# Two edits in a chain of eight layers: the quantised layer's fp32 matmuls as fp32r triples, and the totals of the output projections in parts of 2 and 6 batches

## The chip, the cores and the metric

The kernel runs on one core of one Trainium2 chip. The metric is the device time of one launch in microseconds (us). The core's engines are named as in the profile: PE is TensorE's matmul, PEld its weight load, DVE VectorE, ACT ScalarE, POOL GpSimd, and SP the engine that issues most DMAs. PSUM is the memory that TensorE writes its sums to, in banks of 512 fp32 columns.

## The reference, cut to what matters

The network is a stream x of 8 sequences of 512 tokens and 256 features, to which four attention layers and four feed-forward layers are added in turn. The first feed-forward layer is the quantised one. All its activations are rounded to a grid of 16 bits that is set by the largest absolute value of the whole tensor, and its weights to 4 bits in blocks of 32:

```
def act_qdq(x):
    scale = max(max(abs(x)) / 32767, 1e-12)
    return clip(round(x / scale)) * scale

h    = act_qdq(layernorm(x))                        # 4096 tokens x 256
gate = act_qdq(h @ lpbq_dequant(w_gate).T)          # 4096 x 768
up   = act_qdq(h @ lpbq_dequant(w_up).T)            # 4096 x 768
sig  = round(sigmoid(gate) * 65536), at most 65535, / 65536
act  = act_qdq(gate * sig)
y    = act_qdq(act * up) @ lpbq_dequant(w_down).T   # 4096 x 256
```

Each maximum is over the whole tensor, so a stage can't start before the one ahead of it has ended.

Each attention layer ends in an output projection: the unnormalised heads are multiplied by the reciprocals of the softmax totals (16 or 8 heads for each token), and then by a 256 x 256 matrix, and the result is added to x.

## The kernel before, in words

The program is a row of phases. Each ends in a barrier of all engines, so phases don't overlap and their times add up. Within a phase every engine has its own program, in an order written out by hand, and waits on semaphores. NB is 8 batches of S = 512 tokens, KT = 2 halves of the 256 features, FT = 6 tiles of 128 hidden features, P = 128 and W2 = 256.

**The quantised layer** is these phases. `f1w` (`dequantise`, line 1311) loads the three weights, rounds them on DVE, then transposes them in 36 blocks of 128 x 128 on PE, each copied out of PSUM by ACT (lines 1360 and 1366). `f1n` normalises, `f1g`, `f1h`, `f1i` and `f1j` turn maxima into scales, `f1t` rounds and transposes the activations into `gridT` (code name xT). `f1a` does the gate and up products, PE in tiles of 128 x 512 (lines 1404 and 1408), two fp32 matmuls for each tile; ACT copies each gate tile to the tensor `hidden` (code name act_, line 1417), DVE takes the maximum of each up tile (line 1425) and, for each batch, of the gate tiles (line 1429). The up product isn't kept. `f1b` rounds the gate, takes its sigmoid on ACT, rounds that on DVE and multiplies (lines 1449 to 1464). `f1c` does the up product again, in half batches of 256 tokens: PE (line 1515), ACT scales each tile out of PSUM and adds MAGIC (a float that makes the addition round to a whole number, line 1527), ACT the same for the gated hidden values (line 1528), DVE subtracts MAGIC and scales both (lines 1544 and 1546), multiplies them (line 1552) and takes the maximum (line 1539). `f1d` is the down product. In `f1a` and `f1c` the loops over batches are loops on the engines (`Fori`).

**The output projection** (`outproj`, line 958) runs four times, as `o0`, `o1`, `o3` and `o7`. SP loads the totals in two parts, batch 0 and batches 1 to 7. DVE takes the reciprocals of a part and splits them in an upper and a lower half in fp32r (`split`, lines 1106 to 1110; both parts stand ahead of all its other work), SP writes the halves to DRAM (`spread`, line 1017) and reads them back with heads on partitions (`collect`, line 1022). PE spreads each batch's rows over the features by matmuls with `sel` (`spread`, line 1046), DVE multiplies the heads by them (`scale`, line 1117), ACT rounds that to fp32r (line 1075), DVE subtracts to get the lower half (`lower`, line 1122), and PE multiplies (`project`, line 1056). PE's order is `spread(0)`, then for each b `spread(b + 1)` and `project(b)`. DVE's is `split(0)`, `split(1)`, `scale(0)`, `lower(0)`, and for each b `scale(b + 1)`, `add(b - 1)`, `lower(b + 1)`. The feature halves of a batch of heads are loaded to `xT`, which has three buffers (`load`, line 1007).

## Time and profile before

| | |
|---|---|
| time, median of 3 runs | 5969.54 us (5959.56 to 5976.63) |
| the profiled execution: its own time | 5963.57 us |
| its span | 5961.9 us |
| PE busy | 4522.7 us (76%) |
| DVE busy | 3866.3 us (65%) |
| ACT busy | 2895.7 us (49%) |
| POOL busy | 2017.2 us (34%) |
| moved by DMA | 648.19 MB, 109 GB/s on average |

The shares of busy time are averages over many phases with different limits, so what a change in one phase is worth is read in that phase. The profiled execution took 1.7 us more than its span. The granted clock of TensorE is given as a share of 2.4 GHz: 1.00 is 2.4 GHz, 0.50 is 1.2 GHz, and a figure between them is a stretch with both.

### The profile page before, as it was taken

The numbers are of one execution on the slowest core, as the hardware profiler recorded it, in microseconds if no ns is written. First come the engines' busy times: TensorE is split into PE (matmuls) and PEld (weight loads), VectorE is DVE, ScalarE is ACT, GpSimd is POOL, SyncE is SP. The second block draws the span as 40 slices with busy tenths as digits, with TensorE's granted clock in tenths as the row PEclk, the third lists the DMA queues.
The fourth block names the chain that finished last, engine by engine and source line by source line (L and its number), as shares of the span: only waits on it lengthen the run. The fifth ranks groups of instructions, "written<-read, shape, count | busy, mean of one in ns | idle before, by whom it ended". The sixth has DMA issues, their size and how long they took to land. (4 is left out here: it accounts for less than half of the span.)

```text
span 5961.9 us, 94850 instructions
## 1 busy us (share of the span) xinstructions
PE 4522.7 (76%) x24898; PEld 2823.5 (47%) x24898; DVE 3866.3 (65%) x8219; ACT 2895.7 (49%) x6148; POOL 2017.2 (34%) x3169
## 2 busy tenths in 40 slices
PE   7677764837789739986768676988676987995897
PEld 3333442336433318872236455876455853334434
DVE  6566665395478754443779776569665556885565
ACT  2566642251277533234546566346565324772363
POOL 0344420000366312223435542235541216532342
PEclk9899987969899869997779899999899998997897
DMA  6889950000633202105522321013321044323533
GB/s 224 302 308 309 315 202 16 0 0 5 203 93 93 77 20 65 43 28 135 149 73 110 133 72 42 15 44 124 117 68 32 8 139 130 89 67 113 169 118 102
DMA packets 327033, 648.19 MB, mean 109 GB/s; under 512 B 73202, under 2 KB 140435, under 8 KB 326632
## 3 DMA queue, kind: packets, MB, share of 16 engines
q1 hardware_dynamic: 259544, 463.30, 23.5%
q0 software_dynamic: 67104, 180.70, 10.4%
q8 instruction: 126, 2.06, 0.1%
q14 instruction: 259, 2.12, 0.1%
HBM read 361.41 MB, written 251.28 MB: 103 GB/s over the span
## 5 line engine op out<-in xcount | busy, mean ns | idle before, releaser
L828 DVE TENSOR_REDUCE t_nmax<-t_aps 128x2 f32<-128x1024 f32 x700 | 837.8, 1221 | 278.0 <-PE t_aps L750 272.5
L935 ACT ACTIVATE t_expT<-t_bps 128x512 f32<-128x512 f32 x1290 | 701.3, 599 | 284.9 <-PE t_bps L769 235.1
L769 PE MATMUL t_bps<-t_Q,t_K 51*128 51x512 f32 (+2 forms) x1290 | 526.0, 470 | 60.1 <-ACT t_expT L935 43.9
L750 PE MATMUL t_aps<-t_K,t_Q 49*128 49x512 f32 (+2 forms) x1400 | 465.3, 460 | 63.5 <-DMA t_K<-k_halves 27.9
L769 PEld LDWEIGHTS t_bps<-t_Q,t_K 51*128 51x128 f32 (+2 forms) x1290 | 229.2, 190 | 526.8 <-ACT t_expT L935 373.9
L2112 DVE TENSOR_TENSOR f_hl<-f_h,f_hh 128x512 fp32r<-128x512 f32 x192 | 203.3, 1059 | 409.7 <-ACT f_hh L2037 409.7
L796 PE MATMUL t_ops<-t_expT,t_V 128*17 128x512 f32 (+1 forms) x2560 | 414.4, 615 | 0.4 <-ACT t_expT L935 0.4
L3549 ACT ACTIVATE t_relsb<-t_relsb,t_nmax 128x128 f32<-128x128 f32 (+3 forms) x512 | 288.8, 564 | 221.8 <-DVE t_nmax L3521 221.0
L3427 POOL TENSOR_TENSOR t_relsb<-t_relsb,t_M 128x128 f32<-128x128 f32 x512 | 216.6, 454 | 388.8 <-DMA t_relsb<-rel 388.7
L2404 POOL TENSOR_TENSOR a_crossed<-a_qsb,a_tab 128x256 f32<-128x256 f32 x272 | 262.2, 985 | 251.6 <-ACT a_qsb L2351 218.8
L3180 ACT ACTIVATE t_prob<-t_summed,t_nmax,norms 128x256 f32<-128x256 f32 (+1 forms) x560 | 317.4, 571 | 39.1 <-DVE t_nmax L3239 29.1
L869 POOL DMA_DIRECT2D t_Q<-q_halves x525 | 270.9, 518 | 144.2 <-POOLq L78 74.2
L3456 PE MATMUL t_tps<-ident,t_relsb 128*128 128x128 f32 x1280 | 249.1, 296 | 59.9 <-ACT t_expT L3348 59.8
L3120 PE MATMUL t_tps<-ident,t_prob 128*128 128x128 f32 x964 | 147.6, 298 | 179.3 <-DVE t_prob L3253 179.3
L3521 DVE CUSTOM_DVE_ANT_0 t_relsb<-t_sps,t_relsb 128x128 f32<-128x128 f32 (+3 forms) x512 | 245.9, 482 | 49.3 <-POOL t_relsb L3427 48.9
L869 POOL DMA_DIRECT2D t_K<-k_halves x525 | 267.5, 511 | 17.2 <-issue 8.9
L3468 PE MATMUL t_rps<-t_erk,t_Q 96*128 96x512 bf16 (+3 forms) x512 | 168.4, 332 | 129.9 <-ACT t_rows L3355 69.5
L750 PEld LDWEIGHTS t_aps<-t_K,t_Q 49*128 49x128 f32 (+2 forms) x1400 | 215.0, 199 | 103.0 <-issue 51.7
L3191 ACT COPY t_expT<-t_tps 128x512 f32<-128x512 f32 (+1 forms) x276 | 144.3, 523 | 205.0 <-PE t_tps L3120 205.0
L3456 PEld LDWEIGHTS t_tps<-ident,t_relsb 128*128 128x128 f32 x1280 | 174.7, 153 | 131.8 <-ACT t_relsb L3549 100.1
L1977 PE MATMUL f_yps<-f_wdh,f_hh 128*128 128x256 f32 x768 | 217.7, 283 | 13.8 <-DVE f_hl L2112 13.8
L3348 DVE COPY t_expT<-t_tps 128x128 f32<-128x128 f32 (+1 forms) x256 | 107.9, 422 | 176.1 <-PE t_tps L3456 176.0
(445 smaller groups left out, 12410.3 us busy)
## 6 DMA issues: line engine op xcount, KB each, us to landing
rel<-t_rows SPq DMA_DIRECT2D x128, 640.0 KB, 4.6
t_relsb<-rel SPq DMA_DIRECT2D x128, 640.0 KB, 6.3
t_Q<-q_halves POOLq DMA_DIRECT2D x420, 64.0 KB, 2.5
t_K<-k_halves POOLq DMA_DIRECT2D x420, 64.0 KB, 2.5
k_halves<-a_parts SPq DMA_DIRECT2D x48, 512.0 KB, 4.8
q_halves<-a_parts SPq DMA_DIRECT2D x48, 512.0 KB, 5.6
o_xT<-attended SPq DMA_DIRECT2D x32, 512.0 KB, 4.1
f_R<-combine SPq DMA_DIRECT2D x128, 128.0 KB, 2.9
```

The lines of the kernel that those rows point to most:

```text
L750: last = nc.tensor.matmul(aps[:, (t * PPG + i) % 2, x, :], operand(Qr, KA, p, h, slice(t * P, (t + 1) * P)), operand(Kr, KA, p, h, slice(0 ...
L769: nc.tensor.matmul(bps[:, slot_of(kb, j), :], operand(Kr, KB, p, h, slice(kb * P, (kb + 1) * P)), operand(Qr, KB, p, h, slice(0, S)), star ...
L796: last = nc.tensor.matmul(ops[j * COL:j * COL + VW, :], V[:, p, kb, g * HG + j, :], expT[:, kb % RING, j, :], start=kb == 0, stop=kb == NT ...
L828: nc.vector.tensor_reduce(nmax[:, g, t, i * HPT:(i + 1) * HPT], aps[:, (t * PPG + i) % 2], AX.X, ALU.max, negate=True).then_inc(s["maxed"], 1)
L869: pool.dma_start(dst[o + i * DH:o + (i + 1) * DH, p, cols], rows(src, part, r, g, b)).then_inc(sem, 16)
L935: nc.scalar.activation(expT[:, kb % RING, j, :], bps[:, slot_of(kb, j), :], ACT.Exp).then_inc(s["expo"], 1 + (PAD if end else 0))
L1977: last = nc.tensor.matmul(o, fast(x), fast(w), start=m == 0 and i == 0 and t % 2 == 0, stop=m == NF - 1 and i == 2, skip_group_check=True)
L2404: last = nc.gpsimd.tensor_tensor(y[:, :, k, :], x[:, :, 1 - k, :], tab[:, 2 * i + 1, t, k * HW:(k + 1) * HW].unsqueeze(1).broadcast_to([P, ...
L3180: nc.scalar.activation(prob[:, u.slot, i, x, 0:w], summed[:, u.slot, i, x, 0:w], ACT.Exp, scale=rn[:, ds(u.b * NT + t, 1), h:h + 1].rearra ...
L3456: last = nc.tensor.transpose(tps[:, t % 2, kb * P:(kb + 1) * P], tile(n, t)[:, kb * P:(kb + 1) * P], G.ident[:, :])
L3521: nc.vector.tensor_tensor_reduce(out=tile(n, t), in0=sps[:, u % SB, 0:WIDTH[t]], in1=tile(n, t), scale=1.0, scalar=3.0e38, op0=ALU.add, op ...
L3549: nc.scalar.activation(tile(n, t), tile(n, t), ACT.Exp, scale=-1.0, bias=nmax[:, n % RING, t:t + 1]).then_inc(s["expo"], 1)
```

## The change

**Matmuls.** Where `f1a` and `f1c` multiplied in fp32, each operand now stands in two fp32r parts, the upper one rounded and the lower one the rest, and three fp32r matmuls take the place of one fp32 matmul (upper x upper, lower weight x upper, upper weight x lower; `triple`). The weight parts are made in `f1w`, the upper by ACT's copy and the lower by a subtraction on DVE; the transposes go by groups of three or four to a PSUM bank, with four banks in use instead of two. The activation parts are made batch by batch in `f1a`, and again in `f1c`: the upper by an ACT copy of 128 x 1024 (`upper`), the lower by DVE in chunks of 128 x 512 into a ring of three (`lower`).

**f1a** is unrolled and uses four banks each for gate and up where it used two. **f1b** rounds the sigmoid in one DVE instruction fewer for each half batch. **f1c** works on tiles of 512 tokens, its scales are folded so that the up values need no pass of their own on DVE, and ACT scales the hidden values two batches ahead. **outproj** has parts of 2 and 6 batches, `load(0)` is issued ahead of the weight, and PE waits for the second part at `spread(2)`.

```diff
@@ outproj
-        PARTS = ((0, 1), (1, NB))
+        PARTS = ((0, 2), (2, NB))
...
                 totals(0)
+                load(0)
                 sp.dma_start(W[:, :, :], w).then_inc(s["w"], 16)
                 totals(1)
-                spread(0)
-                load(0)
-                collect(0)
                 if bias is not None:
                     sp.dma_start(B[:, :], bias.broadcast_to([P, D])).then_inc(s["b"], 16)
+                spread(0)
+                load(1)
+                collect(0)
                 spread(1)
-                load(1)
+                load(2)
                 collect(1)
-                load(2)
...
-                    if b < 2:
-                        pe.wait_ge(s[f"rows{b}"], 16)
+                    for i, (first, _) in enumerate(PARTS):
+                        if b == first:
+                            pe.wait_ge(s[f"rows{i}"], 16)
@@ dequantise
-        wps = ps("wps", [P, 2, S])
+        wps = ps("wps", [P, 4, S])
...
+                for n, (srcs, hi, lo) in enumerate(turns()):
+                    if lo is not None:
+                        dve.wait_ge(s["copied"], n + 1)
+                        nc.vector.tensor_tensor(lo.bitcast(F32R), wps[:, n % 4, 0:len(srcs) * P], hi, ALU.subtract).then_inc(s["lower"], 1)
...
+                for n, (srcs, hi, lo) in enumerate(turns()):
+                    if n >= 4:
+                        pe.wait_ge(s["lower" if n - 4 < 8 else "copied"], n - 3)
+                    for m, src in enumerate(srcs):
+                        last = nc.tensor.transpose(wps[:, n % 4, m * P:(m + 1) * P], src, G.ident[:, :])
+                    last.then_inc(s["turned"], 1)
@@ quantised_ffn, helpers of f1a and f1c
+        def triple(pe, s, o, wh, wl, xh, xl, b, m):
+            cols = slice(m * P, (m + 1) * P)
+            for i, (w, k) in enumerate(((wh, 0), (wl, 0), (wh, 1), (wl, 1))):
+                nc.tensor.matmul(o, fast(w[:, k, cols]), fast(xh[:, b % 2, k]), start=i == 0, stop=False)
+            for k in range(KT):
+                if m == 0:
+                    pe.wait_ge(s["lo"], b * KT + k + 1)
+                last = nc.tensor.matmul(o, fast(wh[:, k, cols]), fast(xl[:, (b * KT + k) % 3]), start=False, stop=k == KT - 1)
+            return last
+        def lower(dve, s, xh, xl, c):
+            b, k = divmod(c, KT)
+            if b < NB:
+                dve.wait_ge(s["hi"], b + 1)
+                if c >= 3:
+                    dve.wait_ge(s["u"], ((c - 3) // KT + 1) * FT)
+                nc.vector.tensor_tensor(fast(xl[:, c % 3]), xT[:, k, b * S:(b + 1) * S], xh[:, b % 2, k], ALU.subtract).then_inc(s["lo"], 1)
@@ f1a, DVE
+                    for c in range(3):
+                        lower(dve, s, xh, xl, c)
+                    for b in range(NB):
                         for m in range(FT):
...
+                            nc.vector.tensor_reduce(mx[:, 1, n:n + 1], ups[:, n % 4, :], AX.X, ALU.max, apply_absolute_value=True).then_inc(s["u_mx"], 1)
+                        for c in (b * KT + 3, b * KT + 4):
+                            lower(dve, s, xh, xl, c)
...
@@ f1b, DVE
-                            nc.vector.tensor_scalar(sg[:, x], sg[:, x], 65536.0, MAGIC, ALU.mult, ALU.add).then_inc(s["weighed"], 1)
+                            nc.vector.tensor_scalar(sg[:, x], sg[:, x], 65535.0 / 65536.0, MAGIC / 65536.0, ALU.min, ALU.add).then_inc(s["weighed"], 1)
...
-                            nc.vector.tensor_scalar(sg[:, x], sg[:, x], MAGIC, 65535.0, ALU.subtract, ALU.min).then_inc(s["weighed"], 1)
+                            nc.vector.scalar_tensor_tensor(half(i, x), sg[:, x], MAGIC / 65536.0, half(i, x), ALU.subtract, ALU.mult).then_inc(s["weighed"], 1)
...
-                            nc.vector.scalar_tensor_tensor(half(i, x), sg[:, x], 1.0 / 65536.0, half(i, x), ALU.mult, ALU.mult).then_inc(s["weighed"], 1)
@@ f1c, ACT
+                    def upper(b):
+                        if b >= 2:
+                            act.wait_ge(s["u"], (b - 1) * FT)
+                        nc.scalar.copy(fast(xh[:, b % 2]), xT[:, :, b * S:(b + 1) * S]).then_inc(s["hi"], 1)
...
+                    upper(0)
+                    upper(1)
                     act.wait_ge(s["set"], 1)
+                    scaled(0)
+                    scaled(1)
+                    for b in range(NB):
+                        if b:
+                            act.wait_ge(s["product"], b * 2)
+                        for m in range(FT):
...
+                            nc.scalar.activation(up[:, m, :], ups[:, n % 4, :], ACT.Identity, scale=G.quant[:, 1, 1:2], bias=magic[:, 0:1]).then_inc(s["u_cp"], 1)
+                            if m == 1 and 1 <= b < NB - 1:
+                                upper(b + 1)
+                        if b + 2 < NB:
+                            scaled(b + 2)
@@ f1c, DVE
+                    for c in range(3):
+                        lower(dve, s, xh, xl, c)
+                    whole(0, 0)
+                    whole(0, 1)
+                    for b in range(NB):
+                        lower(dve, s, xh, xl, b * KT + 3)
+                        product(b, 0)
+                        product(b, 1)
                         for x in range(2):
+                            if b + 1 < NB:
+                                whole(b + 1, x)
+                            largest(b, x)
+                        lower(dve, s, xh, xl, b * KT + 4)
```

`whole` is one tensor_scalar of 128 x 1536, `product` one scalar_tensor_tensor of 128 x 1536 that also takes MAGIC off the up values, `largest` the maximum of 128 x 1536, each for a half batch.

## Rows read from the trace of the kernel before

**Rows 1.** Windows over f1a and f1c: busy us (count) by engine, PEclk, DMA share, GB/s.

```profile
1005.00:1173.00 168.00, 165.06 (x384) 72.90 (x384) 57.05 (x56) 28.08 (x48) 0.00 (x0) 1.00 0.00 0
...
1283.00:1376.00 93.00, 85.28 (x384) 74.28 (x383) 82.82 (x64) 73.64 (x112) 0.00 (x0) 0.96 0.00 0
```

The engines of a window's row are PE, PEld, DVE, ACT and POOL, in this order. A line of the timeline has the start (us), the duration (us), engine, line, operation, tiles, and in brackets the idle time before it with what ended it.

**Rows 2.** Timeline of f1a: PE's first matmul, its last weight load, the tail.

```profile
1005.41 1.98 PE L1404 MATMUL f1a_gps<-gridT,gateT 128*128 x4 [2.28 <-ACTq L1413]
...
1169.46 0.19 PEld L1408 LDWEIGHTS f1a_ups<-gridT,upT 128*128 128x128 f32 x1 [0.24 <-issue]
...
1170.62 0.69 DVE L1425 TENSOR_REDUCE mx<-f1a_ups 128x512 f32 x1 [2.74 <-PE f1a_ups L1408]
```

**Rows 3.** Timeline of a later layer: fp32r matmuls of 512 columns, weight loads 1 and 9.

```profile
4803.26 0.19 PEld L1963 LDWEIGHTS f_gps<-f_xh,f_wgh 128*128 128x128 f32 x1
...
4805.09 0.19 PEld L1963 LDWEIGHTS f_ups<-f_xh,f_wul 128*128 128x128 f32 x1
```

**Rows 4.** Tile f_hl (ns min/median/max), and groups of ACT lines (busy us, mean ns).

```profile
L2112 DVE TENSOR_TENSOR f_hl<-f_h,f_hh x192: 691/694/2554, 2253.7 to 4807.9; 128x512 fp32r<-128x512 f32 x192
...
L1527 ACT ACTIVATE f1c_up<-f1c_ups,f1c_magic,quant 128x256 f32<-128x256 f32 x96 | 50.1, 560 | 29.1 <-PE f1c_ups L1515 29.1
...
L1477 ACT ACTIVATE hidden<-hidden,f1b_magic,quant (+1 forms) x16 | 25.6, 1653 | 8.2 <-DVE f1b_magic L1466 8.2
...
L2021 ACT CAST f_xh<-f_x 128x1024 fp32r<-128x1024 f32 x16 | 16.8, 1047 | 1.2
```

**Rows 5.** Timeline of f1b, DVE: the pair that the change removes, and the next.

```profile
1213.09 1.82 DVE L1458 TENSOR_SCALAR f1b_sg<-f1b_sg 128x1536 f32<-128x1536 f32 x2
1214.83 3.42 DVE L1461 SCALAR_TENSOR_TENSOR hidden<-f1b_sg,hidden 128x1536 f32 x2
```

**Rows 6.** Timeline of f1c: PE's start, three operations of DVE, its last.

```profile
1282.63 17.65 PE L1515 MATMUL f1c_ups<-gridT,upT 128*128 x69 [112.16 <-PEq L1509]
...
1321.40 1.75 DVE L1552 TENSOR_TENSOR hidden<-hidden,f1c_up 128x1536 f32 x1
...
1323.07 1.01 DVE L1544 TENSOR_SCALAR f1c_up<-f1c_up,quant 128x1536 f32<-128x1536 f32 x1
...
1323.99 1.01 DVE L1546 TENSOR_SCALAR hidden<-hidden,quant  x1
...
1375.05 1.75 DVE L1539 TENSOR_REDUCE mx<-hidden 128x1 f32<-128x1536 f32 x1
```

**Rows 7.** Window of 1 us in f1c, PE alone: busy, then PEclk.

```profile
1287.00:1288.00 1.00, 1.00 (x4) 0.64 0.00 0
```

**Rows 8.** Timeline of transposes: f1w's, its last copies, and f1t's first.

```profile
936.33 14.80 PE L1360 MATMUL f1w_wps<-ident,f1w_raw 128*128 128x128 f32 x36 [32.28 <-DVEq L1340]
...
950.95 0.48 ACT L1366 COPY downT<-f1w_wps 128x128 f32<-128x128 f32 x2 [0.35 <-PE f1w_wps L1360]
...
990.97 3.51 PE L1272 MATMUL f1t_xps<-ident,f1t_rows 128*128 128x128 f32 x16 [39.84 <-DVE f1t_rows L1255]
```

**Rows 9.** Timeline of o0: second reciprocal, lower(0), rows of part 2, project(0).

```profile
859.04 2.95 DVE L1106 RECIPROCAL o_rs<-o_rs 128x448 f32<-128x448 f32 x1 [1.65 <-DMA o_rs<-sums]
...
865.18 1.23 DVE L1122 TENSOR_TENSOR o_xl<-o_xn,o_xh 128x1024 fp32r<-128x1024 f32 x1 [0.68 <-ACT o_xh L1075]
...
871.52 1.19 PE L1046 MATMUL o_rps<-o_rows,o_sel 32*128 32x512 f32 x2 [8.10 <-DMA o_rows<-o_inverse]
...
872.64 0.58 PE L1056 MATMUL o_yps<-o_Wh,o_xh 128*128 128x256 f32 x1
```

**Rows 10.** Timeline of o1: lower(0) and the start of project(0).

```profile
2056.12 2.34 DVE L1122 TENSOR_TENSOR o_xl<-o_xn,o_xh 128x1024 fp32r<-128x1024 f32 x1 [0.68 <-ACT o_xh L1075]
...
2063.38 0.58 PE L1056 MATMUL o_yps<-o_Wh,o_xh 128*128 128x256 f32 x1
```

**Rows 11.** Timeline of o7: the same two.

```profile
5903.90 1.23 DVE L1122 TENSOR_TENSOR o_xl<-o_xn,o_xh 128x1024 fp32r<-128x1024 f32 x1 [0.68 <-ACT o_xh L1075]
...
5908.41 0.58 PE L1056 MATMUL o_yps<-o_Wh,o_xh 128*128 128x256 f32 x1
```

More of the change, by code:

```diff
@@ L1496, in quantised_ffn, with piece @@
         grid(nc, G, "f1i", [mx[:, 3, 0:2 * NB]], [3])
-        with phase(nc, "f1c", "u u_cp pre set whole product") as (s, psb, ps):
-            up = psb("up", [P, 2, FT, W2])
+        with phase(nc, "f1c", "hi lo u u_cp pre set whole product peak") as (s, psb, ps):
+            up = psb("up", [P, FT, S])
+            xh = psb("xh", [P, 2, KT, S])
+            xl = psb("xl", [P, 3, S])
             magic = psb("magic", [P, 1])
+            both = psb("both", [P, 1])
             ups = ps("ups", [P, 4, S])
+            def piece(b, x):
+                return act_[:, :, b * S + x * W2:b * S + (x + 1) * W2]
@@ L1518, in _ @@
                 @block.scalar
                 def _(act):
-                    def batch(b, first=False):
-                        for x in range(2):
-                            if not first:
-                                act.wait_ge(s["product"], b * 2 + x - 1)
-                                alone(act)
-                            for m in range(FT):
-                                act.wait_ge(s["u"], b * (2 * FT) + x * FT + m + 1)
-                                nc.scalar.activation(up[:, x, m, :], ups[:, slots(b, x, m), 0:W2], ACT.Identity, scale=G.quant[:, 1, 1:2], bias=magic[:, 0:1]).then_inc(s["u_cp"], 1)
-                            nc.scalar.activation(half(b, x), half(b, x), ACT.Identity, scale=G.quant[:, 3, 1:2], bias=magic[:, 0:1]).then_inc(s["pre"], 1)
@@ L1530, in _, with upper, scaled @@
-                    act.wait_ge(s["set"], 1)
-                    batch(0, True)
-                    with act.Fori(0, NB - 1) as i:
-                        batch(i + 1)
+                    def upper(b):
+                        if b >= 2:
+                            act.wait_ge(s["u"], (b - 1) * FT)
+                        nc.scalar.copy(fast(xh[:, b % 2]), xT[:, :, b * S:(b + 1) * S]).then_inc(s["hi"], 1)
+                    def scaled(b):
+                        for x in range(2):
+                            nc.scalar.activation(piece(b, x), piece(b, x), ACT.Identity, scale=G.quant[:, 3, 1:2], bias=magic[:, 0:1]).then_inc(s["pre"], 1)
@@ new lines, in _ @@
+                    upper(0)
+                    upper(1)
+                    act.wait_ge(s["set"], 1)
+                    scaled(0)
+                    scaled(1)
+                    for b in range(NB):
+                        if b:
+                            act.wait_ge(s["product"], b * 2)
+                        for m in range(FT):
+                            n = b * FT + m
+                            act.wait_ge(s["u"], n + 1)
+                            nc.scalar.activation(up[:, m, :], ups[:, n % 4, :], ACT.Identity, scale=G.quant[:, 1, 1:2], bias=magic[:, 0:1]).then_inc(s["u_cp"], 1)
+                            if m == 1 and 1 <= b < NB - 1:
+                                upper(b + 1)
+                        if b + 2 < NB:
+                            scaled(b + 2)
@@ L1554, in _ @@
[L1554 to L1558 removed]
+                        nc.vector.tensor_reduce(mx[:, 0, b * 2 + x:b * 2 + x + 1], piece(b, x), AX.XY, ALU.max, apply_absolute_value=True).then_inc(s["peak"], 1)
+                    nc.vector.memset(magic[:, :], MAGIC)
+                    nc.vector.tensor_tensor(both[:, :], G.quant[:, 1, 0:1], G.quant[:, 3, 0:1], ALU.mult).then_inc(s["set"], 1)
@@ new lines, in _, with whole, product @@
+                    dve.wait_ge(s["set"], 1)
+                    def whole(b, x):
+                        dve.wait_ge(s["pre"], b * 2 + x + 1)
+                        nc.vector.tensor_scalar(piece(b, x), piece(b, x), MAGIC, both[:, 0:1], ALU.subtract, ALU.mult).then_inc(s["whole"], 1)
+                    def product(b, x):
+                        dve.wait_ge(s["u_cp"], (b + 1) * FT)
+                        dve.wait_ge(s["whole"], b * 2 + x + 1)
+                        nc.vector.scalar_tensor_tensor(piece(b, x), up[:, :, x * W2:(x + 1) * W2], MAGIC, piece(b, x), ALU.subtract, ALU.mult).then_inc(s["product"], 1)
```

123 lines of the change are left out of this document (49 added, 74 removed).

## The prediction

> **What bounds the kernel now.** I read the page first. Its shares say little here: no engine is busy throughout, and the program is a row of phases with a barrier behind each, so I took the change's phases one by one, each from its windows and its timeline. The chain that ended last covers only the last output projection, and of the quantised layer it says nothing.
>
> In the quantised layer the limits differ. In f1a PE is busy for 165 of the window's 168 us at clock 1.00, DVE for 57 [rows 1], so PE alone sets the time. In f1b PE does nothing, and DVE's records stand end to end. In f1c PE is busy for 85 of 93 us and DVE for 83 [rows 1]: two engines near the limit, so that to relieve one isn't enough. The end of f1w is a relay between PE and ACT over two banks, 36 transposes in 14.80 us [rows 8]. In an output projection the thing to see is a hole: in o0 `lower(0)` has ended at 866.41, and project(0) starts at 872.64, because PE's `spread(1)` stands ahead of it and waits 8.10 us for the rows of the second part [rows 9].
>
> A record is longer than the distance to the next start on the same engine, since instructions overlap. I use the distance, called pitch, wherever I can.
>
> **The change part by part.**
>
> *f1a.* An fp32 matmul of 512 columns is two records. 384 weight loads run from 1005.41 to 1169.46 [rows 2], a pitch of 164.05 / 383 = 0.428 us, 164.5 us in all. It becomes three records of fp32r, 6 for each of 96 tiles, 576 in all. The trace has the very form: eight steps between nine weight loads take 1.83 us [rows 3], 0.229 us each, so 131.8 us. That is 32.7 us less. Against it: PE waits for the first `upper` (128 x 1024 cast, 1.05 us [rows 4]) and a little for the third chunk of `lower`, 0.3 us. And at every later batch start one chunk is late: chunk 2b + 3 stands behind DVE's last maximum of batch b and its buffer is free only when that batch's matmuls are done. From the end of PE's last slot (1169.46 + 2 x 0.43 = 1170.3) to DVE's start 0.3 us pass, the maximum takes 0.69 [rows 2], the subtraction about 0.67 (record 0.694 [rows 4]), while PE has five matmuls to do meanwhile, 1.14 us. It waits some 0.55 us, seven times: 3.9 us. Behind that wait stand the batch's other tiles, but gate and up have four banks each, so neither ACT nor DVE is held. ACT's casts and DVE's 16 subtractions (11 us in 140) lie beside PE. f1a: -32.7 + 1.35 + 3.9 = -27.5 us. Bounds: -31 if all waits are hidden, -22 if each is twice as long.
>
> A rule of the Trainium skill would make this term larger. Its page "TensorE: Matmul & The Clock Gate", section "Back-to-back issue gap", gives columns / 2.4 + 2.5 ns, 216 ns for 512 columns; the rows of this kernel show 229. By the page f1a would lose 7 us more and the sum would be -77. I keep the rows.
>
> *f1b.* DVE drops one tensor_scalar of 128 x 1536 for each half batch. The pair of a batch costs 1214.83 - 1213.09 = 1.74 us [rows 5], eight times: -13.9 us. The other instructions keep their shapes. ACT has 6.3 us of work in a batch that stays above 10, so nothing new appears. Bounds -12 and -15.
>
> *f1c.* PE's work falls from 85 us to 288 x 0.229 = 66 us, so DVE decides. Its pitches: product 1.67, tensor_scalar 0.92 [rows 6], maximum like the product, its record being 1.75 too. A batch had two of four operations, 10.4 us. It loses two tensor_scalars and gains two subtractions of 0.67: 2 x (1.67 + 1.67 + 0.92 + 0.67) = 9.9 us. The start is longer. ACT does two casts (2.1 us) and four scalings of 1.65 [rows 4], and reaches the first up tile near 1290.7. PE starts near 1283.4 at clock 0.50; the clock rose in the window 1287 to 1288 [rows 7], so the sixth tile is done near 1294, and DVE then does `lower` and can start the first product at 1295.2. From there 7 x 9.9 - 0.7 (the last batches lack a chunk) + 6.8 for the last batch: end 1370.3, against 1375.05 + 1.75 = 1376.8 now [rows 6]. f1c: -6.5 us. Unknown is ACT's activation of 512 columns with scale and bias from memory: 256 take 0.560 and 1536 take 1.653 [rows 4], on a straight line 0.78; the bounds are 0.6 and 1.0. ACT's batch is then 6 x 0.78 + 1.05 + 3.3 = 9.0 us, below DVE's 9.9. Bounds for f1c: -10 and 0.
>
> *f1w.* 36 transposes of 0.22 us at clock 0.50 (16 in 3.51 [rows 8]) are 7.9 us, then a wait and the last copy, 0.8: 8.7 at most, 7.7 if the clock rises on the way as in f1c. Now it is 936.33 to 951.43, 15.1 us. ACT's 11 wide copies and DVE's 8 subtractions, half a microsecond each, run beside it over four banks. f1w: -7.0, bounds -5 and -8.
>
> *Output projections.* The first part grows to two batches, so `spread(1)` no longer waits, and project(0) may start when `lower(0)` is done. `lower(0)` itself comes later: 64 more columns of reciprocal (2.95 / 7 = 0.42 us [rows 9]) and of two copies (0.15), and larger writes and reads, in all 1.2 us, bounds 0.6 and 2.5. Moved too: `load(0)`, 512 KB, goes ahead of the weight and of `totals(1)`, and `load(2)` ahead of `collect(1)`, on SP's queue. That can delay `split(1)`, which stands ahead of `scale(0)` on DVE, by some 1.5 us; but it has one batch less, and `scale(0)` is 1.1 us later anyhow. The gain is project(0)'s start less (end of `lower(0)` + 1.2): o0 872.64 - 867.6 = 5.0 [rows 9]; o1 2063.38 - 2059.7 = 3.7 [rows 10]; o3 has o1's pattern, 3.7; o7 5908.41 - 5906.3 = 2.1 [rows 11]. The wait goes to `spread(2)`, behind project(0), 24 matmuls with half the columns of [rows 3] at half its clock, 0.229 us each, 5.5 us (some 3.5 in o7, whose tiles are narrower). The rows of part two, if they land when they do now (871.5 in o0) or 1 us later, come as project(0) ends. Sum -14.5, bounds -5 and -18.
>
> **Sum.** -27.5 - 13.9 - 6.5 - 7.0 - 14.5 = -69.4 us. The profiled execution took 5963.57 us, so its own after would be 5894. It lies 6 us below the median of the runs, 5969.54, and the same step from the median gives **5900 us**, which I forecast.
>
> **The rivals.**
>
> *The second part is late.* `spread(2)` then waits as long as `spread(1)` did, and the projections gain nothing: -55, 5915 us. For it: 1 MB of loads now precedes or surrounds the totals. Against: nothing of 512 KB lies between `spread(1)` and `collect(1)` that didn't before, bar the change of one load for another.
>
> *f1c hangs on its one up buffer.* ACT may copy a batch only after both products of the one before: six copies and a cast, 5.9 us, beside DVE's 6.2 us until its next product. The margin is 0.3 us and one subtraction. If copies take 1.0 us or PE's tiles come late, a batch takes 11.3: f1c +3.5, in all -59, 5910 us.
>
> *The clock falls at the new waits.* PE now pauses at each batch start, 0.55 us in f1a, some 1.5 in f1c. If the clock fell each time and came back after 5 us, as from 1282.63 to the window of 1287 [rows 6, 7], each fall would cost 2.5 us: 14 falls, 35 us, 5935 us. Against: f1c pauses 8 us in 93 now and shows 0.96 [rows 1], of which the start explains most. The Trainium skill's page named above, section "A second HAM failure mode: psum-queue depth-cycling", describes such a pattern: short pauses between groups of matmuls make the clock swing. By it this rival holds; no row of this trace shows such swings.
>
> *Slower.* The fp32r matmuls run at clock 0.50 throughout f1a and f1c, twice the pitch, 0.458: f1a 576 x 0.458 + 5 - 164.5 = +104; f1c 132 + 8 for its ends, against 94 now, +46; with -35 from the rest, +115, 6085 us. It decides from a pitch of about 0.325 on, where three fp32r matmuls cost 14% more than one of fp32. For it: more weight loads, one for 0.229 us. Against: just that form, with a weight load for each matmul, holds 0.229 [rows 3].
>
> **How the numbers follow.** Chances: the forecast 0.73, part two late 0.08, the up buffer 0.08, the clock's swings 0.08, slower 0.03. The median of three runs moves by 8 us by itself. The forecast's terms at their bounds together give -47 to -82, rarely all at once; with the two near rivals the range is 5884 to 5925, which leaves out the swings, the slower case and the tails. 0.3% (18 us) is about what a measurement of this kernel can tell from no change. Faster by more: 0.95; within: 0.02; slower: 0.03.
>
> **What would show it.** f1a's weight loads at 0.229 us, clock 1.00, seven waits for `lower` of about half a microsecond, and a stage of 138 us from PE's first matmul to its last. f1b's batch at 10.25 us instead of 11.99. f1c with DVE end to end at 9.9 us a batch, PE waiting. f1w's transposes in about 8 us. project(0) of o0 near 5 us after where `lower(0)` now starts plus its length, and a short wait, or none, at `spread(2)`. The prediction fails if f1a's pitch isn't 0.229, if DVE in f1c waits for ACT, or if `split(1)` starts so late that `scale(0)` hangs on it.

## The result

The kernel after takes 5910.0 us (median of 4 runs, 5904.65 to 5919.2), the kernel before, beside it on the same chip, 5970.28 us (4 runs, 5959.56 to 5976.63). The ratio is 0.9896, 95% interval 0.9876 to 0.9916: faster by 60 us. The forecast was 5900, range 5884 to 5925.

The profiled execution of after is the longest of its four, 5919.2 us against 5963.57, so the two profiles differ by 44 us and not by 60. This is where it lies, phase by phase, each from its first instruction to that of the next phase.

| stage | before, us | after, us | difference | forecast |
|---|---|---|---|---|
| f1w | 46.48 | 39.21 | -7.3 | -7.0 |
| f1a | 170.27 | 142.32 | -27.95 | -27.5 |
| f1b | 102.89 | 88.99 | -13.9 | -13.9 |
| f1c | 95.45 | 87.30 | -8.15 | -6.5 |
| o0 | 51.00 | 45.81 | -5.2 | -5.0 |
| o1 | 52.22 | 51.36 | -0.9 | -3.7 |
| o3 | 53.61 | 52.78 | -0.8 | -3.7 |
| o7 | 53.82 | 52.83 | -1.0 | -2.1 |
| split of queries, keys and values ahead of t7 (not touched) | 119.79 | 147.71 | +27.9 | 0 |
| attention t3 (not touched) | 438.14 | 429.04 | -9.1 | 0 |

The touched stages are 65.1 us shorter: the layer 57.3 (forecast 54.9) and the projections 7.9 (forecast 14.5). The untouched rest of this execution is 21 us longer.

### The profile page after: what moved, and what is told of

Its sections match the earlier page's. It is cut to its first block and busy times, and to the rows that moved or that the text cites. A ratio compares the mean times of both kernels' runs of the same rounds, so it can differ in the third digit from the quotient of the medians.

```text
span 5917.5 us, 94345 instructions
## 1 busy us (share of the span) xinstructions
PE 4496.5 (76%) x24994; PEld 2859.1 (48%) x24994; DVE 3860.9 (65%) x8228; ACT 2892.7 (49%) x6091; POOL 2017.6 (34%) x3169
```

## The profile after, beside that of before

The windows over f1a, f1b and f1c, columns as in [rows 1]:

```profile
992.20:1134.50 142.30, 134.70 (x576) 108.59 (x576) 67.32 (x74) 35.73 (x56) 0.00 (x0) 0.99 0.00 1
1138.00:1227.00 89.00, 0.00 (x0) 0.00 (x0) 83.05 (x67) 48.39 (x33) 0.37 (x1) 0.50 0.00 0
1227.10:1314.40 87.30, 71.59 (x288) 55.23 (x288) 78.39 (x67) 65.72 (x72) 0.00 (x0) 0.93 0.00 1
```

f1a has 576 matmuls where it had 384, and PE is busy for 134.7 us where it was for 165.1 [rows 1]. In f1c PE fell from 85 busy us to 72, and DVE, at 78, is the engine near the limit. The granted clock stays at 0.99 and 0.93: TensorE is at its upper level of 2.4 GHz nearly throughout f1a.

Two neighbouring tiles of f1a in the timeline of after:

```profile
1124.03 1.07 PE L1406 MATMUL f1a_gps<-f1a_xh,gateT 128*128 128x512 f32 x4
...
1126.75 1.07 PE L1406 MATMUL f1a_gps<-f1a_xh,gateT 128*128 128x512 f32 x4
```

Between these starts lie one tile of gate and one of up, 12 matmuls in 2.72 us, 0.227 each; the prediction had 0.229 from a later layer [rows 3]. The waits of f1a in the view of waits (us in total, times, longest):

```profile
PEld f1a_gps L1410 <- DVE f1a_xl L1420: 5.0, 8, 0.7
...
PE f1a_gps L1410 <- DVE f1a_xl L1420: 1.8, 7, 0.3
```

There are the seven waits for the chunk that comes late at each batch start (the eighth in PEld's row is at the start of the phase). What one costs stands in neither row: PEld's gives 0.6 us each, PE's idle time 0.26. It is read from start to start. The weight loads of a tile of the first batch, of the tile with the first wait, and of the one behind it:

```profile
1009.82 0.87 PEld L1406 LDWEIGHTS f1a_ups<-f1a_xh,upT 128*128 128x128 f32 x4
...
1011.18 0.87 PEld L1406 LDWEIGHTS f1a_gps<-f1a_xh,gateT 128*128 128x128 f32 x4
...
1012.95 0.19 PEld L1410 LDWEIGHTS f1a_gps<-f1a_xl,gateT 128*128 128x128 f32 x1 [0.68 <-DVE f1a_xl L1420]
1013.06 0.89 PEld L1406 LDWEIGHTS f1a_ups<-f1a_xh,upT 128*128 128x128 f32 x4
```

A tile takes 1.36 us (1009.82 to 1011.18), the one with the wait 1.88: the wait costs 0.52. Over all distances between PE's starts in f1a the seven waits come to 3.6 us.

The start of f1a has a cost that no wait shows. Windows of 2 us near it, PE alone (busy, then clock), in after, in before, and in a second profile of before (experiment 10), in this order:

```profile
995.00:997.00 2.00, 2.00 (x6) 0.50 0.00 0
...
1005.50:1007.50 2.00, 2.00 (x5) 1.00 0.00 0
...
1003.00:1005.00 2.00, 2.00 (x4) 0.50 0.00 0
```

In after some eight matmuls near the start are 0.43 us apart, at the lower level of 1.2 GHz. Before had no such stretch in its first profile and has one in experiment 10.

The timeline of f1c: ACT's first cast, then DVE's first three products.

```profile
1227.10 1.99 ACT L1566 CAST f1c_xh<-gridT 128x1024 fp32r<-128x1024 f32 x2 [12.65 <-PEq L78]
...
1240.03 3.43 DVE L1605 SCALAR_TENSOR_TENSOR hidden<-f1c_up,hidden 128x1536 f32<-128x1536 f32 x2
...
1249.76 3.42 DVE L1605 SCALAR_TENSOR_TENSOR hidden<-f1c_up,hidden 128x1536 f32<-128x1536 f32 x2
...
1259.47 3.43 DVE L1605 SCALAR_TENSOR_TENSOR hidden<-f1c_up,hidden 128x1536 f32<-128x1536 f32 x2
```

The first product starts 13.0 us into the phase, and a batch takes 9.7 us. No bracket stands behind the products: DVE had no idle time ahead of them, so it doesn't wait for ACT's copies.

Now o0, whose rows answer to [rows 9]: the second reciprocal, the two operations of `split(1)` behind it, `lower(0)` and project(0).

```profile
860.20 2.55 DVE L1107 RECIPROCAL o_rs<-o_rs 128x384 f32<-128x384 f32 x1 [2.67 <-DMA o_rs<-sums]
...
862.79 0.36 DVE L1109 CAST o_halves<-o_rs 128x384 fp32r<-128x384 f32 x1
863.18 0.56 DVE L1111 TENSOR_TENSOR o_halves<-o_rs,o_halves 128x384 fp32r<-128x384 f32 x1
...
866.15 1.23 DVE L1123 TENSOR_TENSOR o_xl<-o_xn,o_xh 128x1024 fp32r<-128x1024 f32 x1 [0.68 <-ACT o_xh L1076]
...
867.43 0.58 PE L1057 MATMUL o_yps<-o_Wh,o_xh 128*128 128x256 f32 x1 [2.08 <-DVE o_xl L1123]
```

project(0) waits for `lower(0)` alone. It starts 13.3 us after the start of the phase (854.16), against 18.0 before and a forecast of 12.9: `lower(0)` ends 1.5 us later in the phase than before, where 1.2 was put. The same operations in o1:

```profile
1991.56 2.55 DVE L1107 RECIPROCAL o_rs<-o_rs 128x384 f32<-128x384 f32 x1 [2.52 <-DMA o_rs<-sums]
...
1993.82 18.70 POOL L1099 TENSOR_TENSOR stream<-stream,o_B 128x1024 f32<-128x1024 f32 x7
1994.15 2.24 DVE L1109 CAST o_halves<-o_rs 128x384 fp32r<-128x384 f32 x1
...
1996.42 2.58 DVE L1111 TENSOR_TENSOR o_halves<-o_rs,o_halves 128x384 fp32r<-128x384 f32 x1
1998.92 1.27 DVE L1118 TENSOR_TENSOR o_xn<-o_xT,o_rps 128x512 f32<-128x512 f32 x2
...
2000.88 1.41 DVE L1123 TENSOR_TENSOR o_xl<-o_xn,o_xh 128x1024 fp32r<-128x1024 f32 x1 [0.68 <-ACT o_xh L1076]
...
2002.35 0.58 PE L1057 MATMUL o_yps<-o_Wh,o_xh 128*128 128x256 f32 x1 [5.17 <-DVE o_xl L1123]
```

Here the cast of 128 x 384 takes 2.24 us instead of 0.36, and the subtraction 2.58 instead of 0.56. What differs from o0 is the POOL row: GpSimd adds the bias to the stream, 2.67 us an addition on average (18.70 / 7), from 1993.82 on. The second addition starts at 1996.13 and the third at 1998.55, so those are about the ends of the first and the second. The cast ends at 1996.39 and the subtraction at 1999.00, 0.3 and 0.5 us later: each VectorE instruction looks held until the addition under way is over. `scale(0)` at 1998.92, which has one operand in PSUM, takes its 1.27 us as in o0. o0 has no bias.

That is what the Trainium skill's page "SBUF — State Buffer", section "Who interferes with whom", states: VectorE's second pair of SBUF ports is GpSimd's only one, and who holds it locks the other out; a cast can contend for it, an operation with two SBUF inputs contends with a GpSimd instruction that reads SBUF, and one with at most one SBUF input outside the two-port modes doesn't. The trace agrees: 0.36 to 2.24 us and 0.56 to 2.58 for the first two kinds, 1.27 for `scale`.

## The experiments

Theories for the two gaps. For the projections' missing 6.6 us: (A) GpSimd's bias additions now run beside `split(1)`; (B) the new order of loads eats the gain. They don't exclude each other. For the untouched phases: (C) the granted clock varies there between executions by itself; (D) it hangs on the change.

### 1 and 2: each half of the change alone

```
# experiment 1: before, with outproj() of after
# experiment 2: after, with outproj() of before:
-        PARTS = ((0, 2), (2, NB))
+        PARTS = ((0, 1), (1, NB))
...
-                load(0)
                 sp.dma_start(W[:, :, :], w).then_inc(s["w"], 16)
```

> The kernel before with the edits of outproj alone. The prediction's own term says -14.5 us (5956 us). My theory from the trace after the change says that the four projections gain 5.2, 0.8, 0.8 and 1.0 us, 8 us in all (5962 us), because in the three with a bias GpSimd's additions now run beside the split of the second part. Rival: the projections are slower in some executions for another reason, and the total is at or above that of the kernel before.

> The kernel before with the edits of the quantised layer alone. If the parts add up, the layer's phases are 7.3, 27.9, 13.9 and 8.1 us shorter (transposes, f1a, f1b, f1c), 57 us in all, 5913 us. Rival: something behind the layer gives part of it back each time (in the profiled execution of the changed kernel the projection phase of the last layer, whose code is untouched, took 147.7 us for 119.8), and the total is 30 us shorter only.

The first, the projections alone: 5970.12 us (12 runs) against 5975.82, ratio 0.9988 (0.9969 to 1.0008), which can't be told from no change. The phases are clearer: 45.69, 51.16, 53.04 and 52.69 us, 8.1 less than before. The second, the layer alone: 5895.83 us (6 runs), ratio 0.9872 (0.9843 to 0.9901), with 38.92, 142.15, 89.00 and 87.20 us for f1w, f1a, f1b and f1c. Most of the gain is the layer's, and in the phases the halves don't disturb each other. The whole of the second is 80 us below before (5975.82), where its phases give 57.8 and 5913 us were expected; the interval reaches down to 59. Experiments 3 and 11 lie 79 and 71 us below the runs of before beside them, where their phases give 65 and 66. No run isolates the rest; t3 (below) is 7 us of it in the profile of experiment 2. The phase ahead of t7 takes 132.7 us in the first and 119.9 in the second.

### 3: the bias additions held until `lower(1)`

```
+                pool.wait_ge(s["xl"], 2)
                 ...
                 # additions of B to the stream
```

> The changed kernel with one wait more: in outproj GpSimd starts adding the bias only when DVE has done the second batch's lower half. Theory (DVE's short casts and subtractions in the split of the second part are held by GpSimd's additions): the cast of 128x384 goes from 2.24 us to 0.4, the subtraction from 2.58 to 0.6, the multiplication of the first batch starts some 3 us earlier, and o1 and o3 are 2 to 4 us shorter each, o7 0 to 1.5; 6 us in all. Rival (the loads in their new order are late, and the split waits for its totals): o1 and o3 stay at 51.4 and 52.8 us.

In the timeline of o1 the subtraction of `split(1)` is back at 0.56 us, and the additions start behind `lower(1)`, at 1995.37:

```profile
1987.65 0.56 DVE L1112 TENSOR_TENSOR o_halves<-o_rs,o_halves 128x384 fp32r<-128x384 f32 x1
...
1995.37 21.74 POOL L1100 TENSOR_TENSOR stream<-stream,o_B 128x1024 f32<-128x1024 f32 x8 [8.53 <-DVE o_xl L1124]
...
1998.05 1.29 DVE L1119 TENSOR_TENSOR o_xn<-o_xT,o_rps 128x512 f32<-128x512 f32 x2 [2.84 <-PE o_rps L1047]
...
2000.57 2.93 DVE L1124 TENSOR_TENSOR o_xl<-o_xn,o_xh 128x1024 fp32r<-128x1024 f32 x1
...
2005.94 3.22 DVE L1124 TENSOR_TENSOR o_xl<-o_xn,o_xh 128x1024 fp32r<-128x1024 f32 x1
```

The mechanism of (A) is shown: take the additions from beside an operation and it has its short duration again. The hoped gain isn't there: o1, o3 and o7 take 51.93, 52.08 and 53.24 us, 0.3 more than after in sum, because `lower` now takes 2.93 and 3.22 us instead of 1.23. Within the phase the additions only change whom they hold: VectorE is busy for 40.5 us in this o1, 40.3 in that of after, and 34.9 where no addition runs (experiment 5). The whole took 5897.0 us (4 runs), ratio 0.9866 (0.9831 to 0.99).

### 4 and 11: the third chunk of f1a ahead of the last maximum

```
                         for m in range(FT):
                             n = b * FT + m
+                            if m == FT - 1:
+                                lower(dve, s, xh, xl, b * KT + 3)
...
-                        for c in (b * KT + 3, b * KT + 4):
-                            lower(dve, s, xh, xl, c)
+                        lower(dve, s, xh, xl, b * KT + 4)
```

> The changed kernel, with the late chunk of the lower half in f1a subtracted ahead of the batch's last maximum on DVE, where it was behind it. Theory: the wait of PE at each batch start, 0.6 to 0.7 us, seven times, is the maximum's 0.69 us, and goes: f1a 142.3 to 138 us. Rival: the wait is for something else (a semaphore's way, the weights), and f1a stays within 1 us of 142.3.

> The kernel after with the third chunk subtracted ahead of the last maximum in f1a, timed. Its single profile had f1a at 140.16 us against 142.32. If only that changes, the median is 2 us below that of the kernel after and the ratio to before 0.989; the difference to the kernel after is smaller than what the measurement can tell, so only the phase counts: f1a at 139 to 140.5 us again.

f1a fell from 142.32 us to 140.16 and, in the second profile, to 139.10; 138 was expected. PEld's waits in the second:

```profile
PEld f1a_gps L1410 <- DVE f1a_xl L1420: 0.8, 2, 0.5
```

Between PE's starts the seven waits come to 3.6 to 3.8 us in the six profiles without the edit (after, 2, 3, 7, 8, 9) and to 0.4 in the five with it (4, 5, 6, 11, 12): the edit is worth 3.2 us. What differs besides is the stretch at clock 0.50 at the start. The first twenty distances hold 1.4 to 3.0 us beyond 0.227 each, the most in experiments 4 and 6, which hides a third of experiment 4's gain. Timed, the edit gave 5897.81 us (6 runs, 5876.39 to 5922.69), ratio 0.9879 (0.9851 to 0.9906): the runs scatter by more than the edit is worth.

### 5 and 6: the bias additions moved into the attention phase

```
 # grouped_attention, GpSimd, last batch:
+                        if adds:
+                            for x in range(2):
+                                add_bias(g * 2 + x)
 # outproj gets no bias; experiment 6 has besides:
-        PARTS = ((0, 2), (2, NB))
+        PARTS = ((0, 1), (1, NB))
```

Both have experiment 4's edit; experiment 6 has all of before's `outproj`, its order of loads too.

> The changed kernel with the late chunk of f1a ahead of the maximum, and with the additions of the bias moved out of outproj into the last batch of the attention phase ahead of it, where GpSimd has pauses of 11 us. Theory (GpSimd's 22 us of additions cost DVE 6 us wherever they lie beside DVE's operations on SBUF, and DVE in the attention phase reads PSUM): o1 and o3 fall to 46 us (o0, which has no bias, takes 45.7), o7 to about 51, the attention phases stay as they are; 14 us less in all. Rival (o1 and o3 are long because of their loads or their place): they stay above 50 us. Second rival: the attention phases grow by what the projections lose.

> The kernel of e5 with the outproj of the kernel before (parts of 1 and 7, the old order of loads). If GpSimd's additions were what swallowed the change's gain in o1 and o3, these now take 51 us as o0 did before, 5 us more than in e5. If the change of parts never had anything to give there, they take the same as in e5.

o1 of experiment 5:

```profile
1991.61 2.55 DVE L1125 RECIPROCAL o_rs<-o_rs 128x384 f32<-128x384 f32 x1 [2.51 <-DMA o_rs<-sums]
1994.19 0.36 DVE L1127 CAST o_halves<-o_rs 128x384 fp32r<-128x384 f32 x1
1994.59 0.56 DVE L1129 TENSOR_TENSOR o_halves<-o_rs,o_halves 128x384 fp32r<-128x384 f32 x1
...
1998.84 0.58 PE L1075 MATMUL o_yps<-o_Wh,o_xh 128*128 128x256 f32 x1 [2.08 <-DVE o_xl L1141]
```

From the phase's start to project(0) it is 13.2 us here, 16.9 in after, 18.0 in before [rows 10]. The phases, o0, o1, o3 and o7: 45.52, 45.53, 46.44 and 51.54 us with the new projection, 51.20, 51.19, 50.05 and 53.99 with the old one. Without GpSimd beside it the projections' change is worth 5.7, 5.7, 3.6 and 2.5 us, 17.4 in all, against 8 with it: the forecast's 5.0, 3.7, 3.7 and 2.1 lie nearer to the gain of a phase that nobody disturbs. The additions cost the new projection more than the old one: in o1 VectorE is busy for 40.3 us with them and 34.9 without (after, 5), and with the old projection for 37.3 and 35.2 (before, 6).

The time isn't won for the kernel: experiment 5 took 5892.98 us (6 runs), ratio 0.9873 (0.985 to 0.9897). t7 takes 330.15 and 330.07 us in the two runs, 323.9 to 325.2 in all others, so moving o7's additions costs 5.5 us to win 1.2. The second rival, that attention grows by what the projections lose, is right for t7. For t1 (449.62 and 448.02 us) and t3 (434.33 and 439.47) it is weighed at experiment 12.

### 7: f1c with fp32 matmuls

```
-                            triple(pe, s, ups[:, n % 4, :], uh, ul, xh, xl, b, m).then_inc(s["u"], 1)
+                            for k in range(KT):
+                                last = nc.tensor.matmul(ups[:, n % 4, :], uh[:, k, m * P:(m + 1) * P], xT[:, k, b * S:(b + 1) * S], start=k == 0, stop=k == 1)
+                            last.then_inc(s["u"], 1)
```

The casts and subtractions of the stream in f1c go with it, and the lower halves of the up weights are left out of this one product.

> The changed kernel with f1c's product in fp32 again, on tiles of 512 with the folded scales; no upper and lower parts of the activations in f1c. It multiplies by the upper half of the weights alone. Theory (fp32r takes PE off the limit in f1c, and DVE's subtractions take most of that back): 192 fp32 records at 0.43 us are 82 us of PE, DVE has 8.5 us a batch, PE decides, and f1c takes 92 to 94 us against 87.3. Rival (the folding alone made f1c faster): 87 us or less.

The window over its f1c:

```profile
1226.00:1320.50 94.50, 84.07 (x192) 37.08 (x192) 69.86 (x54) 60.49 (x64) 0.37 (x1) 0.95 0.00 0
```

f1c takes 92.47 us, 5.2 more than after and 3.0 less than before. DVE is relieved to 70 busy us, and PE, at 84, decides. So tiles of 512 and fewer VectorE operations alone give 3 us, and the cheaper matmuls, with the casts and subtractions that they need, the other 5. The reverse, cheaper matmuls with the old VectorE operations, wasn't run; that it would give little is argued from DVE's 83 busy us of 93 before [rows 1].

### 8, 9 and 10: parts and order of loads apart, and before once more

```
 # experiment 8: after with
+        PARTS = ((0, 1), (1, NB))
 # experiment 9: after with the loads of before
                 totals(0)
-                load(0)
                 sp.dma_start(W[:, :, :], w).then_inc(s["w"], 16)
                 totals(1)
-                if bias is not None:
-                    sp.dma_start(B[:, :], bias.broadcast_to([P, D])).then_inc(s["b"], 16)
                 spread(0)
-                load(1)
+                load(0)
                 collect(0)
+                if bias is not None:
+                    sp.dma_start(B[:, :], bias.broadcast_to([P, D])).then_inc(s["b"], 16)
                 spread(1)
-                load(2)
+                load(1)
                 collect(1)
+                load(2)
 # experiment 10: before, nothing changed
```

> The changed kernel with the parts of the kernel before, batch 0 and batches 1 to 7, but the new order of the loads. Theory (the gain of o0 is that project(0) no longer waits for the second part): o0 is back at 50 to 52 us. Rival (the earlier loads alone bring it): o0 stays at 45.8.

> The kernel after, with its larger first part, but with the loads in the order of before: load(0) behind spread(0), the bias behind collect(0), load(2) last. It completes the square with before (old parts, old order: o0 51.00 us, o1 52.22, o3 53.61, o7 53.82) and the run with old parts and new order (54.33, 53.66, 53.53, 56.39). Theory one, the order only costs and the parts alone give the gain, and the two add: o0 45.8 - 3.3 = 42.5 us, o7 near 50.3. Theory two, the new order costs only where the first part is small, because there spread(1) waits for rows that the early loads delay; with the larger part nothing waits for them: o0 45.5 to 46.5, the same as the kernel after. Rival three, the larger part needs the early load of the attention's output, because project(0) now starts earlier than a late load(0) lands: o0 47 us or more. o1 and o3 tell less, since GpSimd's additions run beside VectorE there.

> The kernel before, profiled a second time as a control, nothing changed. If the granted clock of the phases that the change doesn't touch varies by itself, the split of queries, keys and values ahead of t7 takes between 119.8 us (clock 0.81) and 147.7 (0.63), attention t3 between 429 and 444, and either may differ from the first profile of this kernel (119.8 and 438.1). If it hangs on the kernel, they stay within 1 us of the first profile. The phases of the change repeat in both cases: f1a 170.3, f1b 102.9, f1c 95.5, f1w 46.5, o0 51.0, each within 0.7 us.

| o0, us | loads of before | loads of after |
|---|---|---|
| parts of 1 and 7 batches | 50.10 to 51.20 (before, 2, 6, 10) | 54.33 |
| parts of 2 and 6 batches | 45.44 | 45.52 to 45.81 (after, 1, 3, 4, 5, 7, 11, 12) |

The new order costs 3.1 us or more with the old parts, where experiment 8 expected 50 to 52 us, and 0.1 to 0.4 with the new ones. For o0 experiment 9's theory two holds: project(0) of its o0 starts 13.0 us after the phase's start (854.40 to 867.42), in after 13.3 (854.16 to 867.43), although W is cast 3.5 us after the phase's start instead of 5.3. Nothing that decides waits for the early load.

In o1 the order of loads does decide something. From experiment 9's timeline:

```profile
1988.01 0.36 DVE L1109 CAST o_halves<-o_rs 128x384 fp32r<-128x384 f32 x1
1988.40 0.56 DVE L1111 TENSOR_TENSOR o_halves<-o_rs,o_halves 128x384 fp32r<-128x384 f32 x1
...
1992.10 22.70 POOL L1099 TENSOR_TENSOR stream<-stream,o_B 128x1024 f32<-128x1024 f32 x8
...
1995.58 0.58 PE L1057 MATMUL o_yps<-o_Wh,o_xh 128*128 128x256 f32 x1 [2.93 <-DVE o_xl L1123]
```

With the loads of before, `split(1)` starts 4.3 us into o1 and the additions 10.9 us; with those of after it is 6.1 and 8.4. Only in the second case do they meet: `split(1)` isn't held in experiment 9, and project(0) starts 14.4 us into the phase instead of 16.9. Of these 2.5 us o1 keeps 0.5, and the additions now hold `lower`, for up to 3.23 us; o3 and o7 are 1.7 and 1.1 us shorter. So (B) isn't refuted: the new order sends the additions onto `split(1)`, and by this one profile it costs 3.6 of the missing 6.6 us over the four phases. For o7 that is clear of the spread (51.75 against 52.69 to 52.90 in five profiles), for o1 and o3 it isn't (o3 took 51.14 in experiment 7). The order of loads brings nothing in any of these profiles.

The second profile of before repeats f1w, f1b and f1c (46.55, 103.08 and 95.56 us). f1a is 1.9 us longer (172.16), which is the stretch at clock 0.50, and o0 0.9 us shorter, both more than was expected of a repetition. Its o1 takes 55.92 us against 52.22: one profile of o1 is no measure of a microsecond. Over three profiles of the old projection beside GpSimd's additions (before, 2, 10) the four phases sum to 211.8 us on average; over five of the new one (after, 1, 4, 7, 11) to 203.2: the gain is 8.6 us. Experiments 4 and 6 to 10 are one execution each (5878.44, 5929.62, 5916.39, 5897.21, 5903.24 and 5955.35 us), so only their phases are read.

For (C) and (D), the phase ahead of t7 in windows of 10 us, first in after:

```profile
5417.00:5427.00 10.00, 10.00 (x36) 7.98 (x36) 3.69 (x7) 2.07 (x4) 0.00 (x0) 0.50 0.41 157
...
5437.00:5447.00 10.00, 9.41 (x53) 6.97 (x52) 6.00 (x18) 3.51 (x6) 1.26 (x2) 1.00 0.71 264
5447.00:5457.00 10.00, 8.90 (x48) 6.67 (x47) 6.17 (x16) 3.51 (x5) 1.26 (x2) 0.94 0.72 264
5457.00:5467.00 10.00, 10.00 (x35) 7.98 (x35) 3.92 (x8) 3.06 (x5) 0.00 (x0) 0.50 0.45 172
```

and in experiment 10:

```profile
5458.70:5468.70 10.00, 10.00 (x36) 7.98 (x36) 2.73 (x4) 2.57 (x4) 0.00 (x0) 0.50 0.41 157
5468.70:5478.70 10.00, 9.37 (x48) 6.96 (x47) 5.50 (x17) 3.26 (x5) 1.27 (x2) 0.92 0.29 107
```

The same code does 53 matmuls in 10 us at clock 1.00 and 35 or 36 at 0.50, which is 1.2 GHz. Over the whole phase, 119.7 to 120.3 us go with a clock of 0.81 (before, 2, 4, 5, 8, 10, 12), 132.5 to 133.0 with 0.72 (1, 3, 9, 11), 139.6 with 0.68 (6) and 147.7 to 147.8 with 0.63 (after, 7). The levels don't follow the change: experiment 1, with the old layer, has 0.72, experiments 2 and 12, with the new one, 0.81, and experiment 11, which is experiment 4's kernel, has 132.9 us where that had 119.7. Experiment 10 alone would have said the opposite: both untouched phases came within 1 us of the first profile of before. So the 27.9 us of the table are this execution's clock: (C) holds for this phase.

For t3 it stays open. Its clock is 0.91, 0.91 and 0.89 in the three profiles with the old layer (438.1, 437.6 and 444.1 us), and 0.92 or 0.93 in seven of eight with the new one and the bias additions left in place (429.0 to 430.9; the eighth, experiment 7, has 0.91 and 440.8). That may be chance, or have to do with what ran before; no run here tells it.

### 12: the best candidate

```
 # experiment 5, but t7 and o7 as in after: additions moved for o1 and o3 alone
```

> The kernel after with the third chunk of f1a ahead of the last maximum, and with the bias additions of o1 and o3 alone moved to the last batch of the attention ahead; those of o7 stay, since t7 grew by 5.5 us for 1.2 gained in o7. Theory: o1 45.5 and o3 46.5 us, o7 52.8, t7 back at 324 to 325, so that it beats the run with all three moved by 4 us and the kernel after by some 6 to 9: 5885 to 5892 us, ratio 0.986. Rival: t1 and t3 grow by what o1 and o3 win (t3 434 instead of 429 to 431), and it equals the kernel after less the 2 us of f1a, ratio 0.989.

It took 5885.26 us (5 runs, 5876.71 to 5898.05), ratio 0.9862 (0.984 to 0.9884), the lowest median of those with several executions, yet its interval overlaps that of after. The phases: o1 45.93 and o3 45.98 us, 7.9 and 7.0 less than in experiment 11, which ran beside it; t1 448.25 and t3 439.15, 7.8 and 8.5 more. t7 is back at 324.4. The rival looks right: attention takes what the projection wins. The three profiles with moved additions (5, 6, 12) have 448.6 us for t1 and 437.6 for t3 on average, the eight others with the new layer 442.6 and 431.3, and that is as much as o1 and o3 win. But one profile without moved additions has 450.1 us for t1 (experiment 1), so the clock alone can do as much. In the windows over t1 VectorE is as busy as without (351.8 us against 351.7) and GpSimd for 20 us more (290.5 against 270.8), while PE's clock is 0.90 against 0.92. Whether the additions or the clock made t1 and t3 longer isn't settled by that; t7, at a clock of 0.93 against 0.94, is the case where the additions' 5.5 us came twice.

## Why the prediction was right, and where it was wrong

**f1a** was right by its own steps, with one term missing. The pitch was 0.227 us instead of 0.229, worth 1.1 us more. The seven waits came as described and cost 3.6 us, 0.52 each, against 3.9. Missing was the start: the matmuls at clock 0.50 and the waits for the first chunks hold 1.9 us there, where 0.3 was put. The phase lost 27.95 us against a forecast of 27.5. That the profiled execution of before had no such start is chance: experiments 10 and 1, with the old f1a, have one of 1.8 us and take 172.2 and 172.0 us, so against them the gain is 1.7 to 1.9 us larger. The Trainium skill's page "TensorE: Matmul & The Clock Gate", section "Back-to-back issue gap", gives columns / 2.4 + 2.5 ns for an isolated matmul. That is 0.216 us, too low for this stream of them, as the rows said.

**f1b** was a pair of records removed from a chain that stands end to end: 13.9 forecast, 13.90 measured, 13.9 to 14.1 in all.

**f1w** was forecast from the transposes' pitch at clock 0.50, 7.0 against 7.3 measured.

**f1c** started as forecast (13.0 us to the first product against 13.1, a 512-column activation of 0.78 us, the value taken off the straight line). The period was mis-sized, 9.72 us instead of 9.86, since a subtraction takes 0.60 us from start to start and not 0.67; that is 1.0 of the 1.6 us that the phase gained beyond its forecast. Another 0.6 is a chunk more that is missing at the end: the last period lacks two subtractions, and the prediction took off one. Experiment 7 shows what PE's share in it is.

**Output projections**: this is the step that failed, 7.9 us (8.6 over several profiles) instead of 14.5. In o0 it was right to 0.2 us. The step is that `split(1)`, delayed by some 1.5 us, costs `scale(0)` nothing because it has one batch less, so that `lower(0)` comes 1.2 us later and no more. In o1 `split(1)` starts 1.8 us later and the additions 1.3 us earlier, they meet, the two copies of `split(1)` take 4.8 us together instead of 0.9, and `scale(0)` stands behind them. `lower(0)` ends 3.75 us later in the phase. That is one of the prediction's own signs of failure, `scale(0)` hanging on `split(1)`, and in o1 and o3 it came. The warning stood in the rows shown: `lower(0)` takes 2.34 us in o1 [rows 10] and 1.23 in o0 [rows 9], same line, same shape. The prediction took the first as given and didn't ask which operation would be hit once the additions and `split(1)` moved against each other. Experiments 3, 5 and 6 show that the additions are the missing part, and experiment 9 that the order of loads has a share in where they fall.

**The rivals.** "Part two late" did not come: `spread(2)` stands right behind project(0) in o1, at 2007.76, its weight load after 0.22 us of idle time. "The up buffer" did not: behind its start, DVE doesn't wait in f1c. "The clock falls at the new waits" did not: 0.99 in f1a with seven waits, and 0.227 us from matmul to matmul again behind each. The pattern that the Trainium skill's page "TensorE: Matmul & The Clock Gate" describes in its section "A second HAM failure mode: psum-queue depth-cycling" doesn't appear in this phase. The prediction's remark that no row of the trace of before shows the clock swing was wrong, though: in windows of 10 us over the phase ahead of t7 it is 1.00 from 5499, 0.50 from 5519 and 0.93 from 5529. "Slower" needed a pitch of 0.325 us. The rival that was missing is the one that happened, contention between VectorE and GpSimd, at 6 us of the forecast's gain.

**The total** came within the range, and 65 us of the forecast 69 came in the phases named. It is partly luck that it lies so near: the projections' miss of 6.6 us is offset by 2.4 that the layer gave beyond its forecast, and phases that the change doesn't touch vary by 20 us and more between executions, while the median moved by 60. One sum of the prediction is off: its terms at their lower bounds give -44 us (22 + 12 + 0 + 5 + 5), not -47.

## What to carry to other kernels

Cost a step per stage and per neighbour: when one line has two durations in the trace of before, find out who runs beside it, and ask whom the change will put there. Where two engines are both near the limit, an edit for one of them is worth only the distance to the other, 3 of 8 us in experiment 7. When a whole-kernel time scatters by 20 us, read the phases that an edit touches and compare those, and profile the unchanged kernel twice before an untouched phase is explained.

## What the runs showed of the hardware

- Beside GpSimd's additions in SBUF, 2.3 to 3.4 us each, a VectorE cast of 128 x 384 took 2.24 us instead of 0.36, a subtraction of two SBUF operands 2.58 instead of 0.56, and one of 128 x 1024 up to 3.45 instead of 1.23; a multiplication with one operand in PSUM kept its 1.27.
- TensorE, busy for 8.9 to 10 of every 10 us, went from clock 1.00 to 0.50 and back in one phase, in other places in each execution: 119.7 to 147.8 us for the same instructions.
- Neither engine's idle time is the cost of a wait of TensorE: seven waits had 0.68 us each ahead of the weight load and 0.25 ahead of the matmul, and cost 0.52 each from start to start; 3.2 of these 3.6 us were won when the chunk came earlier.
- The same f1a began with or without a stretch at clock 0.50: 0.1 us lost to it in one profile of before, 1.8 in two others with the old f1a.
- Three fp32r matmuls in place of one of fp32, with a weight load each, took 0.227 us each for 512 columns at clock 1.00 (the median of 576) and 0.43 at 0.50.
